# Masks of a sliding-window attention layer: added to the scores on TensorE instead of cut out of the probabilities on GpSimd

## The reference, cut to what matters

```
i, j = rows, columns
scores  = einsum('bthd,bshd->bhts', q, k_win) * (1 / sqrt(hd))
allowed = (j <= i) & (j >= i - WINDOW)            # WINDOW = 64
scores  = where(allowed, scores, finfo.min)
window_out = softmax(scores) @ v_win
combined = concat([linear_out, window_out])
x = x + combined @ Wout
```

## Time and profile before

| | |
|---|---|
| median of 3 runs | 2486.41 us (2482.18 to 2491.59) |
| the profiled execution | 2491.9 us, of it the span 2490.2 us |
| busy in the span: PE / DVE / ACT / POOL | 2088.4 / 1473.3 / 1142.6 / 739.9 us |
| mean granted clock of PE | 0.922 of full speed |
| window layer | from about 1140 to 1760 us of the span |

### The profile page before, as it was taken

One profiled execution on the slowest core, in us unless ns is written; L12 is line 12 of the kernel. 1 busy time (PEld: TensorE's weight loads), 2 busy tenths in 40 slices (PEclk: granted clock), 3 DMA queues, 4 the chain that ended last, 5 costly groups with the idle time before them and its releaser, 6 DMA issues. The chain is left out here.

```text
span 2490.2 us, 39452 instructions
## 1 busy us (share of the span) xinstructions
PE 2088.4 (84%) x14978; PEld 1389.5 (56%) x14978; DVE 1473.3 (59%) x3209; ACT 1142.6 (46%) x1673; POOL 739.9 (30%) x848
## 2 busy tenths in 40 slices
PE   3599899999899288955788889788799995899989
PEld 1243343343443277844456455465577774788989
DVE  6586686686674455455535535445267875566555
ACT  1065555555467255412443434426245554355444
POOL 1014114113112233202532524515211100266556
PEclk9599999999999698977878899899899997999999
DMA  4803503503500100018260530610222222000000
GB/s 134 122 2 67 93 1 71 89 1 74 86 1 1 41 1 0 0 35 150 57 107 1 106 54 19 121 22 2 97 83 80 85 90 68 1 14 14 14 14 18
DMA packets 77747, 126.54 MB, mean 51 GB/s; under 512 B 16641, under 2 KB 34817, under 8 KB 77569
## 3 DMA queue, kind: packets, MB, share of 16 engines
q1 hardware_dynamic: 76032, 123.86, 23.8%
q10 hardware_dynamic: 1536, 0.26, 0.1%
HBM read 93.52 MB, written 30.31 MB: 50 GB/s over the span
## 5 line engine op out<-in xcount | busy, mean ns | idle before, releaser
L922 DVE TENSOR_REDUCE nmx<-banks 128x1 f32<-128x192 f32 (+4 forms) x1216 | 581.0, 518 | 313.3 <-PE banks L696 305.7
L836 ACT ACTIVATE probs<-banks 128x1024 f32<-128x1024 f32 (+3 forms) x512 | 462.2, 937 | 402.2 <-PE banks L717 401.1
L636 POOL TENSOR_SCALAR_AFFINE_SELECT probs<-probs 128x512 f32<-128x512 f32 (+2 forms) x432 | 267.9, 626 | 856.7 <-ACT probs L836 844.6
L717 PE MATMUL banks<-qs,ks 97*128 97x128 bf16 (+4 forms) x1856 | 338.6, 300 | 84.2 <-DMA qs<-nmT 75.4
L696 PE MATMUL banks<-ks,qs 96*128 96x192 bf16 (+6 forms) x1408 | 389.2, 310 | 4.6 <-DVE nmx L922 3.0
L739 PE MATMUL banks<-probs,v 128*17 128x256 f32 (+6 forms) x3712 | 320.5, 429 | 11.7 <-POOL probs L636 11.1
L717 PEld LDWEIGHTS banks<-qs,ks 97*128 97x128 bf16 (+1 forms) x1856 | 162.9, 106 | 186.1 <-DMA qs<-nmT 87.8
L696 PEld LDWEIGHTS banks<-ks,qs 96*128 96x128 bf16 x1408 | 140.1, 101 | 112.8 <-DVE nmx L922 44.6
L694 PE MATMUL banks<-below,identb 128*128 128x128 bf16 x512 | 117.1, 231 | 27.8 <-DMA ks<-zk 17.5
L694 PE MATMUL banks<-near,identb 128*128 128x192 bf16 (+1 forms) x512 | 117.9, 260 | 26.3 <-DMA ks<-zk 17.6
L694 PEld LDWEIGHTS banks<-below,identb 128*128 128x128 bf16 x512 | 50.6, 99 | 153.1 <-DVE nmx L922 101.3
(11 more groups left out here) (211 smaller groups left out, 3491.9 us busy)
## 6 DMA issues: line engine op xcount, KB each, us to landing
ks<-zk SPq DMA_DIRECT2D x192, 137.6 KB, 8.2
qs<-zq SPq DMA_DIRECT2D x192, 128.0 KB, 4.9
fs_masked<-in_fside SPq DMA_DIRECT2D x32, 616.0 KB, 3.7
zk<-parts SPq DMA_DIRECT2D x48, 275.2 KB, 2.5
zq<-parts SPq DMA_DIRECT2D x48, 256.0 KB, 5.2
mk_masked<-in_mask SPq DMA_DIRECT2D x32, 154.0 KB, 3.9
x_tokens<-in_x SPq DMA_DIRECT2D x4, 1024.0 KB, 8.4
out<-x_tokens SPq DMA_DIRECT2D x32, 128.0 KB, 1.7
```

The costliest lines, as they stand in the source:

```text
L636: pool.affine_select(out=v, in_=v, compare_op=ALU.is_ge, fill=0.0, base=const, pattern=[[0, QH], [by_c, wd]], channel_multiplier=by_p).the ...
L717: ins = pe.matmul(banks[0:nk, at + side, o:o + n], ks[0:kr, q, 2 * pair + side, key:key + nk], qs[0:kr, q, 2 * pair + side, q0:q0 + n], st ...
L836: ins = act.activation(dst, src, ACT.Exp, scale=DH ** -0.5)
L922: dve.tensor_reduce(dst, src, AX.X, ALU.max, negate=True).then_inc(emptied_v, 1)
```

## The change

The masks of the window layer's steps are dropped, so POOL has no affine_select there. For every piece of a step with an exponential, PE first writes the mask by a matmul with the identity as weights, through which as many columns of `near_k` move as the piece has queries (`near_k` is a 128 x 256 table of 0 and -1e30, built on POOL at the start); the score matmul adds to it. The exponential then gives zero there. `values` waits for `probs_ready` instead of `masked`, by the unchanged lines above. The causal layer's masks stay as they are.

```diff
     one = Step("exp", (((0, 1), 0, ((here, 0, 0, HALF),)),), ((here, 0, 0, HALF, True),),
-               ((0, P, 0, -1, 1), (WINDOW, HALF - WINDOW, 0, 1, -1)))
+               ())
     pieces, gives = [(after, P, P, P)], [(after, P, P, P, False)]
-    masks = [(P, P, 0, -1, 1), (P + WINDOW, P - WINDOW, 0, 1, -1)]
     if c:
         pieces.append((before, WINDOW, 0, WINDOW))
         gives.append((before, WINDOW, 0, WINDOW, False))
-        masks.append((WINDOW, WINDOW, WINDOW - P, 1, -1))
-    return [one, Step("exp", (((0, 1), 0, tuple(pieces)),), tuple(gives), tuple(masks)), lin]
+    return [one, Step("exp", (((0, 1), 0, tuple(pieces)),), tuple(gives), ()), lin]
...
+        near_k = sb(whole, "near_k", [P, 2 * P], BF16)
...
-            for m in (below, near):
+            for m in (below, near, near_k):
                 pool.memset(m[:], 0.0).then_inc(filled, 1)
...
+            pool.affine_select(out=near_k[:], in_=near_k[:], compare_op=ALU.is_ge, fill=MASKED, base=0,
+                               pattern=[[1, 2 * P]], channel_multiplier=-1).then_inc(const_ready, 1)
+            pool.wait_ge(const_ready, 5)
+            pool.affine_select(out=near_k[:], in_=near_k[:], compare_op=ALU.is_ge, fill=MASKED, base=WINDOW,
+                               pattern=[[-1, 2 * P]], channel_multiplier=1).then_inc(const_ready, 1)
...
                                     o, q0 = p_ * HALF + col - base, c * ch + query
+                                    past = q0 - P * (blk - 1)
+                                    cover = not first and blk and one.func == "exp"
+                                    if cover:
+                                        pe.matmul(banks[0:nk, at + side, o:o + n], identb[:], near_k[:, past:past + n],
+                                                  start=True, stop=False, skip_group_check=True)
                                     ins = pe.matmul(banks[0:nk, at + side, o:o + n],
                                                     ks[0:kr, q, 2 * pair + side, key:key + nk],
                                                     qs[0:kr, q, 2 * pair + side, q0:q0 + n],
-                                                    start=True, stop=True, skip_group_check=True)
+                                                    start=not cover, stop=True, skip_group_check=True)
```

More of the change, by code:

```diff
@@ L104, in window_steps @@
     lin = Step("square", (((0, 1), 0, ((0, 0, 0, HALF),)),), ((0, 0, HALF, HALF, True),), ())
-    one = Step("exp", (((0, 1), 0, ((here, 0, 0, HALF),)),), ((here, 0, 0, HALF, True),),
-               ((0, P, 0, -1, 1), (WINDOW, HALF - WINDOW, 0, 1, -1)))
+    one = Step("exp", (((0, 1), 0, ((here, 0, 0, HALF),)),), ((here, 0, 0, HALF, True),), ())
     pieces, gives = [(after, P, P, P)], [(after, P, P, P, False)]
-    masks = [(P, P, 0, -1, 1), (P + WINDOW, P - WINDOW, 0, 1, -1)]
     if c:
@@ L219, in build @@
         sem("x_loaded"), sem("loaded")
-        arriving = setup(nc, a, sem, x, ident, identb, below, near, ctxT)
-        attention_layer(nc, a, sem, sb, x, ident, identb, below, ctxT, banks, True, arriving)
+        arriving = setup(nc, a, sem, x, ident, identb, below, near, near_k, ctxT)
+        attention_layer(nc, a, sem, sb, x, ident, identb, below, near_k, ctxT, banks, True, arriving)
         mlp(nc, a, sem, sb, x, ident, banks)
-        attention_layer(nc, a, sem, sb, x, ident, identb, near, ctxT, banks, False)
+        attention_layer(nc, a, sem, sb, x, ident, identb, near, near_k, ctxT, banks, False)
         masked_context(nc, a, sem, sb, x, ident, identb, ctxT, banks)
@@ L231, in clear, with setup @@
     nc.all_engine_barrier(sems_to_clear=range(min(numbers), max(numbers) + 1))
-def setup(nc, a, sem, x, ident, identb, below, near, ctxT):
+def setup(nc, a, sem, x, ident, identb, below, near, near_k, ctxT):
     first_loaded, x_loaded, filled, const_ready = map(sem, ("first_loaded", "x_loaded", "filled", "const_ready"))
@@ L250, in _ @@
             pool.memset(identb[:], 0.0).then_inc(filled, 1)
-            for m in (below, near):
+            for m in (below, near, near_k):
                 pool.memset(m[:], 0.0).then_inc(filled, 1)
-            pool.wait_ge(filled, 4)
+            pool.wait_ge(filled, 5)
             for m in (ident, identb):
@@ L262, in _ @@
                                pattern=[[1, P + WINDOW]], channel_multiplier=-1).then_inc(const_ready, 1)
-            pool.wait_ge(const_ready, 4)
+            pool.affine_select(out=near_k[:], in_=near_k[:], compare_op=ALU.is_ge, fill=MASKED, base=0,
[3 more added lines that the diff above has]
+                               pattern=[[-1, 2 * P]], channel_multiplier=1).then_inc(const_ready, 1)
             pool.affine_select(out=near[:], in_=near[:], compare_op=ALU.is_ge, fill=MASKED, base=WINDOW,
@@ L395, in wait_free, with attention_layer @@
             pe.wait_ge(*self.counts[n])
-def attention_layer(nc, a, sem, sb, x, ident, identb, mask, ctxT, banks, first, arriving=()):
+def attention_layer(nc, a, sem, sb, x, ident, identb, mask, near_k, ctxT, banks, first, arriving=()):
     eps = 1e-5 if first else 1e-6
```

## The result

| | before | change |
|---|---|---|
| median | 2484.3 us (4 runs, 2481.6 to 2491.6) | 2506.2 us (4 runs, 2501.2 to 2510.1) |
| ratio | 1 | 1.0082, 95% interval 1.0049 to 1.0115 |
| the profiled execution | 2491.9 us | 2501.2 us, of it the span 2499.5 us |
| mean granted clock of the profiled execution | 0.922 | 0.932 |

By the ratio the change makes the kernel 0.8% slower: 20 us, by the interval 12 to 29. The forecast was 29.6 us, 2516 us, with a range of 2490 to 2538.

What follows compares the result with a forecast made beforehand. PE was taken as the bound, 526 of 620 us busy in the changed layer. 49.4 + 5 - 8.5 - 6.3 - 12 + 2 = 29.6 us on the 2486.4 us median gives 2516 us; range 2490 to 2538.

Steps and rivals of the forecast that it cites:

- the shift's DMA: Third group of a batch: PE's wait for the small DMA carrying the maxima grows in three batches, +2 us.
- the clock: Window layer: denser full-width mask matmuls turn 24 of 136 us at half clock to full clock, -12 us.
- Added on PE: Window layer: 704 mask matmuls on PE at 0.11, 0.06 and 0.03 us each at full clock, +49.4 us.
- The half-clock premium: Window layer: part of the mask matmuls runs at half clock and costs twice, +5 us, bounds 0 and 10.9.
- The rival that the clock pays for it: Window layer: mask matmuls keep the array active in most half-clock stretches, -25 us; 12 us slower, 2498 us; chance 0.18.
- Tails: Ends of batches, without ring work: 11 chunks hide their 0.8 us of mask matmuls in PE's mask wait, -8.5 us.
- POOL's queue: Projection of the next batch: POOL's subtractions no longer queue behind masks, saving PE 2.64 us in three batches, -6.3 us.
- The mask chain everywhere: All 64 chunks: step `one`'s two masks stand in the exponential-to-values chain, 78 us go; 24 less, 2463 us; chance 0.05.

Runs made afterwards that it cites:

- the narrower step: Step `one` over 192 queries instead of 256, second step's value matmuls unchanged: 0.9931 on the kernel before; 1.0032 on the changed kernel, both against before.
- the new order: Kernel before with three of the projection's subtractions ahead of the masks in POOL's own order, batches 1 to 3: 0.9979, -5 us.

## Why the prediction was right

The direction and the mechanism hold: the mask matmuls cost their full distance between starts on PE, and only what PE waited for POOL comes back. The sum of 29.6 us was 9 too high (the interval of the measurement is 12 to 29). Two terms carry that: the shift's DMA, with the wrong sign, 6 to 7 us off, and the clock, which gave back 2 to 6 us more than its two terms said. Term by term:

- **Added on PE, +49.4:** right. The last batch's second group shows 3.0 us for 3.1, and 3.0 once more when the matmuls are doubled; the medians of the doubled kernel give 46 to 50. The 0.081 us for a pair at 128 columns, which the Trainium skill gives (TensorE: Matmul & The Clock Gate, Back-to-back issue gap), does not hold in this stream: 0.05 to 0.06.
- **The half-clock premium, +5, and the clock, -12:** together -7; the runs show -9 to -13. The mean granted clock is 0.9295 in the four runs of the change and 0.9243 in the 77 of before that ran beside the experiments, not beside the change. That is 2 x 0.0052 x 2500 = 26 us less at half clock, 13 us of time, or 9 by the spread of the runs of before. The -12 was called a choice, and that it came so near is luck. The premium rested on half-clock stretches staying as long as they were; they did not, with all 16 waits for the shift's DMA still there.
- **The rival that the clock pays for it:** the trace pair looks like it. There the layer has 51 us less at half clock, so up to 25 us of time, the rival's own amount, and the two executions differ by 9.3 us for the rival's 12. Its after has the highest clock of the four runs of the change, and its before is in the lower third of what before shows. In the mean of the runs the amount is half of that or less, so it happens in single executions and not in the mean.
- **Tails, -8.5, and POOL's queue, -6.3:** about right. In the pair PE's waits for masks (11.1 us) went for 3.2 more of `oT`, so 7.9, and the waits for `whole`, 7.9, went altogether, where about 0.5 us had been expected to stay in batch 1: 15.8 for 14.8. Without any masks 22 us go (15 to 29), of which the profiled execution shows 16 in these waits and 7 in those for the DMA. The mechanisms are the ones named. The tail's chunk is at 4.65 us for a forecast of 4.5. (The forecast's own product, 11 chunks of 0.8 us, is 8.8 and not 8.5.)
- **The shift's DMA, +2:** wrong sign. At the three places that the forecast named, the wait fell by 4.3 us in sum, where it was to grow by 2; within the bounds of 9 given. The cause is open: all 16 waits come to 38.9 us without any masks, 40.7 with the narrower step, masks on POOL and the new order, 43.7 with doubled mask matmuls, 46.7 with masks on both engines. One execution of each kernel does not tell POOL's queue from chance.
- **The mask chain everywhere (faster):** ruled out. In the last batch's first three groups the price of the matmuls is paid in full, with nothing gained, and without any masks 22 us go, not the 78 of this rival.

The forecast had named three signs of being wrong, and all three are in the profiled pair: the layer is 7.2 us longer and not at least 15, its clock is 0.94 and so over 0.93, and the tail's chunk is 4.65 us and not 4.4 to 4.6. The first two are one and the same thing, the clock of two single executions, by which a difference of 30 us in the layer can't be judged; the third is the wait for `oT`, 0.15 us a chunk more than reckoned. The pair's own terms come to 49.4 - 7.9 - 7.9 - 4.6 - 25 = 4 us with the clock at its full worth, against the 7.2 seen.

## What to carry to other kernels

Work moved off an idle engine brings only what the busy engine waited for it, and costs its full price in the busy engine's stream; price it there by the distance between starts, and look at the busiest engine's waits by releaser before moving anything. Waits for a side engine that does two kinds of work can be a matter of the order in its queue, which costs nothing to change. And before finding a cheaper home for a mask, ask whether the masked part needs to be computed: the 64 columns that the window never reaches were worth 17 us (11 to 24).

## What the runs showed of the hardware

The time of one and the same program goes with the clock that was granted. Over the 25, 29 and 23 runs of the kernel before, the mean granted clock was between 0.915 and 0.931 and the time between 2471.5 and 2507.1 us, with correlations of -0.84, -0.93 and -0.91 and 17 to 18 us for each 0.01. Counting 0.01 as 50 us less at half clock and 25 us of time, as above, reads high against this. A pair of executions can so show half or twice the effect of a change that is worth 0.8%, and a comparison of two traces should begin with their clocks. A stretch in which PE is busy for nearly all of its time can be at half clock: 15.58 of 15.6 us with a granted clock of 0.51. It begins where PE had waited 3.07 us for the shift's DMA. The same tail with full-width mask matmuls in it stood at 0.69 with 15.33 us busy. That looks like what the Trainium skill says (TensorE: Matmul & The Clock Gate, Part 1), that activity releases the throttle, but it can't be put down to the mask matmuls: in the kernel with POOL's new order alone, whose program on PE is that of before, the same tail stood at 0.80, with less PE time in it because each matmul was shorter:

```profile
1261.80:1277.40 15.60, 13.88 (x148) 7.38 (x148) 2.59 (x12) 9.46 (x12) 8.28 (x14) 0.80 0.53 68
```

What ties the clock to the mask matmuls are the means of many runs (0.929 against 0.923 with the narrower step), and not one stretch of one trace.
